# The query's row normalisation moved behind the third gate, its split behind the fourth Silu

## The chip, the cores and the metric

The kernel runs on one core of a Trainium2 chip. A core has five engines with queues of their own: TensorE (PE), VectorE (DVE), ScalarE (ACT), GpSimd (POOL) and SyncE (SP, here the queue of all DMAs). The metric is the device time of one execution in microseconds, the median of several runs. Lower is better.

## The reference

32 batches of `x` and of a context, each 256 x 512. For a batch:

```python
# attention-like mixing over channels; q is x with normalised rows
p = Wp @ q;  g = Wg @ ctx;  t = Wt @ ctx
att = sum over a group of 32 channels and all columns of p * g, * 0.125
u = Wz (per group) @ (att * t)
u = (u - mean) / sqrt(var + eps) * gamma + beta     # over a group
x1 = x + ctx + u
# feed-forward over rows; Q is blockwise FP4 quantisation, blocks of 16
n = layernorm(x1)
h = silu(Q(n) @ Q(w_gate).T) * (Q(n) @ Q(w_up).T)   # 512 -> 1408
out = x1 + Q(h) @ Q(w_down).T                       # 1408 -> 512
```

## The kernel before

The 256 rows of a batch (a "context", numbered i) make two tiles of 128 rows, the even one (s = 0) and the odd one (s = 1); tile j = 2i + s. After a stretch in which the weights are quantised, turned and split, the kernel is one loop over contexts, and each engine has the order of its work written out by hand in a function `body(i)`. Only semaphores join the engines. Each engine works strictly in its own order: an instruction that waits holds up all that stands behind it.

Products with more precision than one 16-bit pass are made of pieces: a matrix is split into a high part and a low part (`hi`, `lo`), and TensorE sums three products. The high part is made by ScalarE (a cast), the low part by VectorE or GpSimd (value minus high part).

What belongs to a tile j in `body`:

- TensorE: the scores of tile j + 2 (p, g, u), then the hidden product of tile j in four quarters of 352 columns, each gate and up side by side (L463), the group means (L450) and group spread of tile j + 2 between them, then the output product of tile j - 1 (L474).
- ScalarE: for each quarter the Silu (L711); between them moments of u, the split `c_hi` of the context after next (L630), `xm` (L640, an absolute value for the rounding), `x_hi` (L619), `q_hi` (L635), and behind the fourth Silu `affine`, which writes `v_sb` (L609).
- VectorE: a gate for each quarter (L916: Silu times up); the quantisation of the next tile's rows between the gates (`normalise2` L828, maximum L763, scale L766, reciprocal L839, `x_y` L742, then `x_finish` L751, L755, L759, and `x_lo` L906); `copy_group` L800 and `variance` L806 for the attention part; and in the odd tile `normalise1` (L785, two instructions, one for each half of the context after next), which writes `q`. Behind the fourth gate comes the quantisation of h: maximum L763, `h_scale` L766, small instructions up to L876, `h_y` L742; then `residual` L814, which needs `v_sb`, the statistics of x1, and `emit` L925.
- GpSimd: in the odd tile `ctx_lo` (`c_lo`, L1122), `columns` (five one-column instructions, L1136 to L1142, once `copy_group` is done), `q_lo` (L1128, once `q_hi` is done), `columns_affine` (five one-column instructions, L1146 to L1154, once `variance` is done, feeding `affine`), then `root2` and `add_ctx` (`xc`, L1117).

The semaphores that the moved work touches: `q_norm` (VectorE's L785; ScalarE's `q_hi` and the load of the next x wait for it), `q_hi_done` (GpSimd's `q_lo` waits), `q_ready` (TensorE's scores wait for `q_lo`).

Of the kernel before, what the change touches and what calls it, by code (L numbers as in the profile page):

```python
# [40 lines left out]
def at_least(eng, sem, n):  # L41

    if isinstance(n, int) and n <= 0:
        return
    eng.wait_ge(sem, n)
# [10 lines left out]
def build(nc, x, ctx_in, Wt, Wp, Wg, Wz, gamma, beta, w_gate, w_up, w_down, out):  # L56
# [18 lines left out]
    with ExitStack() as stack:  # L75
# [247 lines left out]
        def final_sets(c):  # L323

            return FINAL[2 * c:2 * c + 2]
# [257 lines left out]
        def _(act):  # L583
            def copy_p(t, pair):
                act.wait_ge(p_done, t + 1)
                at_least(act, pg_summed, t)
                nc.scalar.copy(p_sb[:, :], pairs[:, pair, 0, :]).then_inc(p_copied, 1)

            def copy_u(t):
                act.wait_ge(u_done, t + 1)  # L590
                at_least(act, v_ready, t)
                nc.scalar.activation(u_sb[:, :], ubank[:, :], ACT.Identity, accum_out=u_sum[:, 0:1]).then_inc(u_copied, 1)

            def u_moments(t):
                at_least(act, grp_done, t)
                at_least(act, sq_steps, 2 * t)
                act.wait_ge(u_copied, t + 1)
                nc.scalar.activation(rowst[:, 1:2], u_sum[:, 0:1], ACT.Identity, scale=-1.0 / D).then_inc(u_mean_made, 1)
                act.wait_ge(u_mean_made, t + 1)
                nc.scalar.activation(u_dev[:, :], u_sb[:, :], ACT.Square, bias=rowst[:, 1:2],  # L600
                                     accum_out=u_sum[:, 1:2]).then_inc(u_squared, 1)
                act.wait_ge(u_squared, t + 1)
                nc.scalar.activation(rowst[:, 2:3], u_sum[:, 1:2], ACT.Identity, scale=1.0 / D).then_inc(rowst_ready, 1)

            def affine(t):

                act.wait_ge(aff_steps, 8 * t + 8)
                at_least(act, x1_ready, t)
                nc.scalar.activation(v_sb[:, :], u_sb[:, :], ACT.Identity, bias=att[:, 10:11],  # L609
                                     scale=att[:, 8:9]).then_inc(v_ready, 1)  # L610
# [5 lines left out]
            def x_hi(t):  # L616
                act.wait_ge(xq_ready, t + 1)
                at_least(act, x_turned, 16 * t)
                nc.scalar.copy(xq_parts[:, 0, :], xq[:, :]).then_inc(x_hi_done, 1)  # L619

            def h_hi(j):
                at_least(act, h_turned, 16 * j)
                for r, (a, b) in enumerate(HPIECES):
                    act.wait_ge(hq_ready, 2 * j + r + 1)
                    nc.scalar.copy(hq_parts[:, 0, a:b], hq[:, a:b]).then_inc(h_hi_done, 1)  # L625

            def ctx_hi(b):
                act.wait_ge(c_loaded, 16 * b + 16)
                at_least(act, u_done, HT * b)
                nc.scalar.copy(c_parts[0][:, :, :], c_in[:, :, :]).then_inc(c_hi_done, 1)  # L630

            def q_hi(b):
                act.wait_ge(q_norm, HT * b + HT)
                at_least(act, p_done, HT * b)
                nc.scalar.copy(q_parts[0][:, :, :], q[:, :, :]).then_inc(q_hi_done, 1)  # L635

            def grain(m, y, y_done, count, done):

                act.wait_ge(y_done, count)
                nc.scalar.activation(m, y, ACT.Abs, scale=GRAIN).then_inc(done, 1)  # L640

            def weights_hi(weight_set):
                k, _, cols, dst = weight_set
                split_hi(dst[0], k % 2, len(cols), w_turned, k + 1, w_hi_done)
# [50 lines left out]
            def body(i):  # L695
                ahead = not isinstance(i, int) or i + 2 < NB
                more = not isinstance(i, int) or i + 1 < NB
                for s in range(HT):
                    j = HT * i + s
                    first = isinstance(j, int) and j == 0  # L700
                    if more and not first:
                        copy_p(j + 2, s)
                        copy_u(j + 2)
                    if not first:
                        h_hi(j - 1)
                    for c in range(GROUPS):
                        act.wait_ge(gu_done, GROUPS * j + c + 1)
                        at_least(act, h_done, GROUPS * j + c - 1)
                        if first and c == 0:
                            act.wait_ge(w_q_done, 3 * WCH - 1)  # L710
                        nc.scalar.activation(silu[:, c % 2, :], pairs[:, (s + 1 + c) % 2, 0, 0:GW], ACT.Silu,  # L711
                                             scale=w_unit[:, 0:1]).then_inc(silu_done, 1)
                        if first:
                            for one in final_sets(c):
                                weights_hi(one)
                        if c == 0 and more and not first:
                            u_moments(j + 2)
                        if c == 0 and ahead and s == 1:
                            ctx_hi(i + 2)
                        if c == 1 and (more or s == 0):  # L720
                            grain(xm[:, :], xn[:, :], x_y_done, j + 2, x_grain_done)
                        if c == 1 and ahead and s == 1:
                            q_hi(i + 2)
                        if c == 1 and (more or s == 0):
                            x_hi(j + 1)
                        if c == 3 and more:
                            affine(j + 2)
                    grain(hm[:, :], h[:, :], h_y_done, j + 1, h_grain_done)
# [10 lines left out]
        def _(dve):  # L739
# [143 lines left out]
            def h_snap_add(j):  # L883
                dve.wait_ge(h_grain_done, j + 1)
                snap_add(h[:, :], hm[:, :], h_t_done)

            def h_snap_back(j):
                dve.wait_ge(h_t_done, j + 1)
                snap_back(h[:, :], hm[:, :], h_r_done)
# [132 lines left out]
            def body(i):  # L1022
                more = not isinstance(i, int) or i + 1 < NB
                ahead = not isinstance(i, int) or i + 2 < NB
                for s in range(HT):
                    j = HT * i + s
                    t = j + 2
                    first = isinstance(j, int) and j == 0
                    quant_x = more or s == 0
                    if not first:  # L1030
                        h_snap_add(j - 1)
                        h_snap_back(j - 1)
                    if more:
                        sum_pg(t, s)
                    if not first:
                        h_finish(j - 1)
                        h_lo(j - 1)
                    for c in range(GROUPS):
                        gated(j, s, c)
                        if first:  # L1040
                            for k, _, cols, dst in final_sets(c):
                                split_lo(dst[1], dst[0], k % 2, len(cols), w_hi_done, k + 1, w_lo_done)
                        if c == 0 and quant_x:
                            normalise2(j + 1)
                            x_first(j + 1)
                            x_scales(j + 1)
                            x_y(j + 1)
                        if c == 0 and ahead and s == 1:
                            normalise1(i + 2)
                        if c == 1 and more:  # L1050
                            copy_group(t)
                        if c == 1 and quant_x:
                            x_finish(j + 1)
                        if c == 3 and more:
                            variance(t)
                        if c == 2 and quant_x:
                            x_lo(j + 1)
                        if c == 2 and ahead and s == 0:
                            ln1(i + 2)

                    h_first(j)
                    h_scales(j, s)
                    h_units(j, s)
                    h_y(j)
                    if more:
                        residual(t, s)
                        x1_moments(t)
                        x1_mean(t)
                    if not first:
                        emit(j - 1, 1 - s, 16 * (i - 1) if s == 0 else 16 * i)  # L1070
# [193 lines left out]
```

## Time and profile before

| what | value |
|---|---|
| median of 3 runs | 1893.15 us (1892.28 to 1893.98) |
| the profiled execution | 1893.97 us, span 1892.2 us |
| TensorE matmul busy | 1742.4 us (92%) |
| VectorE busy | 1656.3 us (88%) |
| GpSimd busy | 805.8 us (43%) |
| ScalarE busy | 719.6 us (38%) |
| mean granted TensorE clock | 0.978 of full speed |

The span is what the trace covers; the execution's time is 1.8 us more. A row of the timeline gives the start in microseconds from the span's start, the duration, the engine, the line in the kernel, the operation, the written tile, an arrow and the read tiles, and the shapes; "x2" is two like instructions in a row, given as one. In brackets stands how long the engine had been idle and what ended it. In the rows, `x` is the program's x1, and `att`, `ln_mv` and `ln_rs` lose their numbers. A waiting instruction is shown in two ways: where it waits for a semaphore there is idle time ahead of it, and where it has been issued and then can't go on, its own duration is longer.

### The profile page before, as it was taken

To read this page: it belongs to the slowest core of one execution; us is meant where nothing else is said; L and a number is where in the kernel's file an instruction comes from. 1 tells how busy PE (TensorE), PEld (TensorE's weight loads), DVE (VectorE), ACT (ScalarE), POOL (GpSimd) and SP (SyncE) were. 2 spreads that over 40 slices of the span, in tenths; PEclk is the share of its full clock that TensorE was granted. 3 is DMA by queue.
4 is the path that set the end of the run, shared out by engine and by line. 5 is a ranking of instruction groups with operands and counts; after the bars stand their busy time and mean duration, and the time that the engine had idled before them with its cause. 6 is when DMAs were issued, how large, how long until landed. Compare 5 with 4: busy or idle time off the path is not lost.

```text
span 1892.2 us, 30546 instructions
## 1 busy us (share of the span) xinstructions
PE 1742.4 (92%) x10062; PEld 1098.9 (58%) x10062; DVE 1656.3 (88%) x2629; ACT 719.6 (38%) x1237; POOL 805.8 (43%) x1065
## 2 busy tenths in 40 slices
PE   1537999999999999999999999999999999999996
PEld 1436566666666666666566666666566666666653
DVE  5585999999999999999999999999999999999984
ACT  2334434333344343433344343433434333433431
POOL 3648434344444434344444434434344444434400
PEclk9778999999999999999999999999999999999998
DMA  5100232322322232323222233222232233232222
GB/s 192 53 1 17 44 70 69 75 60 61 72 69 63 60 69 70 74 60 68 64 69 70 54 69 75 69 67 68 58 74 70 56 67 69 69 73 61 48 54 47
DMA packets 281879, 123.04 MB, mean 65 GB/s; under 512 B 252928, under 2 KB 254208, under 8 KB 281856
## 3 DMA queue, kind: packets, MB, share of 16 engines
q1 hardware_dynamic: 281856, 122.74, 27.4%
q8 instruction: 13, 0.21, 0.0%
q14 instruction: 10, 0.08, 0.0%
HBM read 43.03 MB, written 16.78 MB: 32 GB/s over the span
## 4 chain that ended last, share of the span: by engine, by line
PE 40%; DVE 35%; issue 16%; ACT 5%; POOL 2%; DVEq 1%; DMA 1%; ACTq 0%; SPq 0%; POOLq 0%
PE pairs L463 19%; PE obank L474 13%; PE pairs L442 4%; DVE hq L759 3%; DVE q L785 3%; DVE h L751 3%; DVE h L916 3%; DVE h L742 3%; ACT early L711 3%; DVE h_amax L763 3%; PE ubank L442 2%; DVE x L814 1%; ACT u_dev L600 1%; DVE ln_st L818 1%; DVE xn L755 1%
## 5 line engine op out<-in xcount | busy, mean ns | idle before, releaser
L463 PE MATMUL pairs<-w_gate_hi,xT_parts 128*128 128x352 f16 x2048 | 629.3, 313 | 16.1 <-DVE h L916 11.7
L463 PE MATMUL pairs<-w_up_hi,xT_parts 128*128 128x352 f16 x2048 | 628.4, 313 | 0.0
L474 PE MATMUL obank<-w_parts,hT_parts 128*128 128x512 f16 x2112 | 468.0, 380 | 12.9 <-DMA hT_parts<-raw 12.9
L474 PEld LDWEIGHTS obank<-w_parts,hT_parts 128*128 128x128 f16 x2112 | 207.5, 100 | 249.3 <-issue 15.9
L463 PE MATMUL pairs<-w_up_lo,xT_parts 128*128 128x352 f16 x1024 | 320.4, 313 | 0.0
L463 PE MATMUL pairs<-w_gate_lo,xT_parts 128*128 128x352 f16 x1024 | 320.3, 313 | 0.0
L463 PEld LDWEIGHTS pairs<-w_gate_hi,xT_parts 128*128 128x128 f16 x2048 | 205.3, 100 | 142.5 <-DVE h L916 23.3
L463 PEld LDWEIGHTS pairs<-w_up_hi,xT_parts 128*128 128x128 f16 x2048 | 200.6, 98 | 97.5
L916 DVE SCALAR_TENSOR_TENSOR h<-pairs,w_unit,early 128x352 f32<-128x352 f32 x256 | 148.1, 579 | 91.0 <-ACT early L711 90.9
L711 ACT ACTIVATE early<-pairs,w_unit 128x352 f32<-128x352 f32 x256 | 141.0, 551 | 86.6 <-PE pairs L463 86.6
L625 ACT CAST raw<-hq 128x704 f16<-128x704 f32 x128 | 99.6, 780 | 183.0 <-DVE hq L759 181.6
L1117 POOL TENSOR_TENSOR xc<-x_in,c_in 128x512 f32<-128x512 f32 x64 | 166.0, 2614 | 0.0
L1122 POOL TENSOR_TENSOR c_lo<-c_in,c_hi 128x512 fp32r<-128x512 f32 x64 | 95.2, 1508 | 161.3 <-ACT c_hi L630 154.3
L1136 POOL TENSOR_TENSOR att<-rowst,grp 128x1 f32<-128x1 f32 x64 | 40.4, 631 | 274.2 <-DVE grp L800 274.2
L640 ACT ACTIVATE hm<-h 128x1408 bf16<-128x1408 f32 x66 | 91.1, 1380 | 150.3 <-DVE h L742 150.3
L1158 POOL TENSOR_TENSOR ln_rs<-ln_mv,eps_col 128x1 f32<-128x1 f32 x64 | 14.9, 232 | 302.6 <-DVE ln_mv L822 302.6
L755 DVE SCALAR_TENSOR_TENSOR h<-hm,h 128x1408 f32<-128x1408 bf16 x66 | 138.2, 2094 | 2.2
L463 PEld LDWEIGHTS pairs<-w_up_lo,xT_parts 128*128 128x128 f16 x1024 | 100.2, 98 | 52.8
L463 PEld LDWEIGHTS pairs<-w_gate_lo,xT_parts 128*128 128x128 f16 x1024 | 100.2, 98 | 52.8
L609 ACT ACTIVATE v_sb<-u_sb,att 128x512 f32<-128x512 f32 x64 | 52.2, 815 | 205.2 <-POOL att L1154 205.2
L759 DVE SCALAR_TENSOR_TENSOR hq<-h,h_unit 128x704 f32<-128x704 f32 x128 | 121.9, 992 | 0.1
L901 DVE TENSOR_TENSOR raw<-hq,raw 128x704 f16<-128x704 f32 x128 | 108.5, 890 | 3.0
(163 smaller groups left out, 3023.6 us busy)
## 6 DMA issues: line engine op xcount, KB each, us to landing
x_in<-in_x SPq DMA_DIRECT2D x32, 512.0 KB, 3.4
c_in<-in_ctx SPq DMA_DIRECT2D x32, 512.0 KB, 3.5
out<-early SPq DMA_DIRECT2D x64, 256.0 KB, 2.1
raw<-in_L_ffn_w_down SPq DMA_DIRECT2D x2, 1408.0 KB, 8.8
raw<-in_L_ffn_w_gate SPq DMA_DIRECT2D x2, 1280.0 KB, 8.4
w_parts<-in_L_ffn_w_up SPq DMA_DIRECT2D x2, 1280.0 KB, 9.1
xT_parts<-raw SPq DMA_TRANSPOSE x64, 3.1
hT_parts<-raw SPq DMA_TRANSPOSE x64, 5.2
```

Source lines behind the costliest of these rows:

```text
L442: mm = pe.matmul(dst, wT[wpart][:, k, s * P:(s + 1) * P], src[part][:, k, :], start=(k == 0 and wpart == 0 and part == 0), stop=(k == HT - ...
L463: mm = pe.matmul(pairs[:, pair, n, 0:GW], xT[s][part][:, k, :], w1[n][wpart][:, k, c * GW:(c + 1) * GW], start=(k == 0 and part == 0 and w ...
L474: mm = pe.matmul(obank[:, :], hT[part][:, k, :], w2[wpart][:, k, :], start=(k == 0 and part == 0 and wpart == 0), stop=(k == KH - 1 and pa ...
L625: nc.scalar.copy(hq_parts[:, 0, a:b], hq[:, a:b]).then_inc(h_hi_done, 1)
L640: nc.scalar.activation(m, y, ACT.Abs, scale=GRAIN).then_inc(done, 1)
L711: nc.scalar.activation(silu[:, c % 2, :], pairs[:, (s + 1 + c) % 2, 0, 0:GW], ACT.Silu, scale=w_unit[:, 0:1]).then_inc(silu_done, 1)
L755: nc.vector.scalar_tensor_tensor(out=y, in0=m, scalar=GRAIN, in1=y, op0=ALU.max, op1=ALU.subtract).then_inc(done, 1)
L759: nc.vector.scalar_tensor_tensor(out=blocks(q_out), in0=blocks(y), scalar=-factor, in1=over_block(scale), op0=ALU.mult, op1=ALU.mult).then ...
L901: nc.vector.tensor_tensor(hq_parts[:, 1, a:b], hq[:, a:b], hq_parts[:, 0, a:b], ALU.subtract).then_inc(h_lo_done, 1)
L916: nc.vector.scalar_tensor_tensor(out=h[:, c * GW:(c + 1) * GW], in0=pairs[:, (s + 1 + c) % 2, 1, 0:GW], scalar=w_unit[:, 1:2], in1=silu[:, ...
L1117: nc.gpsimd.tensor_tensor(xc[:, s, :], x_in[:, s, :], c_in[:, s, :], ALU.add).then_inc(xc_ready, 1)
L1122: nc.gpsimd.tensor_tensor(c_parts[1][:, s, :], c_in[:, s, :], c_parts[0][:, s, :].bitcast(F32), ALU.subtract).then_inc(c_ready, 1)
```

## The change

Two conditions differ. In the odd tile VectorE's `normalise1` of the context after next is issued behind the third gate rather than the first, and ScalarE's `q_hi` behind the fourth Silu rather than the second.

```diff
@@ scalar, body(i), for each quarter c @@
                         if c == 1 and (more or s == 0):
                             grain(xm[:, :], xn[:, :], x_y_done, j + 2, x_grain_done)
-                        if c == 1 and ahead and s == 1:
+                        if c == 3 and ahead and s == 1:
                             q_hi(i + 2)
                         if c == 1 and (more or s == 0):
                             x_hi(j + 1)
@@ vector, body(i), for each quarter c @@
                             x_y(j + 1)
-                        if c == 0 and ahead and s == 1:
+                        if c == 2 and ahead and s == 1:
                             normalise1(i + 2)
                         if c == 1 and more:
                             copy_group(t)
```

VectorE in the odd tile (s = 1), from the scaling of the next rows (L742) to the fourth gate. Before:

```order
L742 SCALAR_TENSOR_TENSOR xn<-xn,x_rinv 128x512
L785 TENSOR_SCALAR q<-x_in,ln_mv,ln_rs 128x512 x2
L916 SCALAR_TENSOR_TENSOR h<-pairs,w_unit,early 128x352
L800 COPY grp<-ubank 128x3
L751 SCALAR_TENSOR_TENSOR xn<-xm,xn 128x512
L755 SCALAR_TENSOR_TENSOR xn<-xm,xn 128x512
L759 SCALAR_TENSOR_TENSOR xq<-xn,x_scale 128x512
L916 SCALAR_TENSOR_TENSOR h<-pairs,w_unit,early 128x352
L906 TENSOR_TENSOR raw<-xq,raw 128x512
L916 SCALAR_TENSOR_TENSOR h<-pairs,w_unit,early 128x352
```

And with the change (`early` holds the Silu, `pairs` are TensorE's PSUM banks):

```order
L742 SCALAR_TENSOR_TENSOR xn<-xn,x_rinv 128x512
L916 SCALAR_TENSOR_TENSOR h<-pairs,w_unit,early 128x352
L800 COPY grp<-ubank 128x3
L751 SCALAR_TENSOR_TENSOR xn<-xm,xn 128x512
L755 SCALAR_TENSOR_TENSOR xn<-xm,xn 128x512
L759 SCALAR_TENSOR_TENSOR xq<-xn,x_scale 128x512
L916 SCALAR_TENSOR_TENSOR h<-pairs,w_unit,early 128x352
L785 TENSOR_SCALAR q<-x_in,ln_mv,ln_rs 128x512 x2
L906 TENSOR_TENSOR raw<-xq,raw 128x512
L916 SCALAR_TENSOR_TENSOR h<-pairs,w_unit,early 128x352
```

The two L785 have passed the second and third gates and the three instructions of `x_finish`.

ScalarE in the same tile, from the second Silu on (L711; `raw<-xq` is `x_hi`). Before:

```order
L711 ACTIVATE early<-pairs,w_unit 128x352
L640 ACTIVATE xm<-xn 128x512
L635 CAST q_hi<-q 128x1024
L619 CAST raw<-xq 128x512
L711 ACTIVATE early<-pairs,w_unit 128x352 x2
L609 ACTIVATE v_sb<-u_sb,att 128x512
```

And with the change:

```order
L711 ACTIVATE early<-pairs,w_unit 128x352
L640 ACTIVATE xm<-xn 128x512
L619 CAST raw<-xq 128x512
L711 ACTIVATE early<-pairs,w_unit 128x352 x2
L635 CAST q_hi<-q 128x1024
L609 ACTIVATE v_sb<-u_sb,att 128x512
```

`q_hi` has passed `x_hi` and the last two Silus and stands next to `affine`. The orders of TensorE, GpSimd and SyncE are the same in both.

## Rows read from the trace of the kernel before

**Rows 1.** Timeline of VectorE: start us, us, engine, line, operation.
```profile
991.67 0.68 DVE L906 TENSOR_TENSOR raw<-xq,raw 128x512 f16<-128x512 f32 x1
...
1044.70 0.68 DVE L906 TENSOR_TENSOR raw<-xq,raw 128x512 f16<-128x512 f32 x1
```

**Rows 2.** Timeline of TensorE, fourth quarter of the odd tile.
```profile
1014.39 0.31 PE L463 MATMUL pairs<-w_gate_hi,xT_parts 128*128 128x352 f16 x1
1014.54 0.31 PE L463 MATMUL pairs<-w_up_hi,xT_parts 128*128 128x352 f16 x1
1015.17 0.32 PE L463 MATMUL pairs<-w_gate_hi,xT_parts 128*128 128x352 f16 x1 [0.32 <-DVE h L916]
```

**Rows 3.** Waits: engine and line, waited for, us, times, longest.
```profile
PE ubank L450 <- ACT rowst L603: 12.9, 30, 0.4
```

**Rows 4.** Timeline of VectorE in the odd tile.
```profile
1011.44 1.30 DVE L742 SCALAR_TENSOR_TENSOR xn<-xn,x_rinv 128x512 f32<-128x512 f32 x1
...
1012.66 1.95 DVE L785 TENSOR_SCALAR q<-x_in,ln_mv,ln_rs 128x512 f32<-128x512 f32 x2
...
1016.53 0.69 DVE L759 SCALAR_TENSOR_TENSOR xq<-xn,x_scale 128x512 f32<-128x512 f32 x1
...
1018.44 0.58 DVE L916 SCALAR_TENSOR_TENSOR h<-pairs,w_unit,early 128x352 f32<-128x352 f32 x1 [1.22 <-ACT early L711]
...
1018.94 1.62 DVE L906 TENSOR_TENSOR raw<-xq,raw 128x512 f16<-128x512 f32 x1
...
1020.49 0.57 DVE L916 SCALAR_TENSOR_TENSOR h<-pairs,w_unit,early 128x352 f32<-128x352 f32 x1
...
1022.75 0.22 DVE L766 TENSOR_SCALAR h_scale<-h_amax 128x88 f32<-128x88 f32 x1
...
1024.17 0.27 DVE L876 TENSOR_SCALAR h_unit<-h_scale,h_pow 128x88 f32<-128x88 f32 x1
...
1024.35 1.62 DVE L742 SCALAR_TENSOR_TENSOR h<-h,h_rinv 128x1408 f32<-128x1408 f32 x1
...
1025.89 0.68 DVE L814 TENSOR_TENSOR x<-v_sb,xc 128x512 f32 x1
```

**Rows 5.** Timeline of GpSimd in the odd tile.
```profile
1010.93 2.94 POOL L1122 TENSOR_TENSOR c_lo<-c_in,c_hi 128x512 fp32r<-128x512 f32 x2 [5.19 <-ACT c_hi L630]
...
1017.52 2.50 POOL L1128 TENSOR_TENSOR q_lo<-q,q_hi 128x512 fp32r<-128x512 f32 x2
...
1021.26 0.19 POOL L1146 TENSOR_TENSOR att<-att,eps_col 128x1 f32<-128x1 f32 x1 [1.25 <-DVE att L806]
...
1022.72 0.19 POOL L1154 TENSOR_TENSOR att<-gb,att 128x1 f32<-128x1 f32 x1
```

**Rows 6.** Line L785, all executions: ns min/median/max.
```profile
L785 DVE TENSOR_SCALAR q<-x_in,ln_mv,ln_rs x64: 533/542/1493, 7.1 to 1756.7; 128x512 f32<-128x512 f32 x64
```

**Rows 7.** Timeline of VectorE and GpSimd while the weights are prepared.
```profile
107.08 2.59 POOL L1182 TENSOR_TENSOR w_parts<-hq,w_scale 128x1408 f32<-128x1408 f32 x1
...
107.93 1.77 DVE L766 TENSOR_SCALAR x_scale<-x_amax 128x32 f32<-128x32 f32 x1
```

**Rows 8.** Timeline of VectorE and GpSimd, start of the odd tile.
```profile
1001.90 1.61 DVE L751 SCALAR_TENSOR_TENSOR h<-hm,h 128x1408 f32<-128x1408 bf16 x1
...
1001.92 1.65 POOL L1107 TENSOR_TENSOR ln_rs<-ln_mv,eps_col 128x2 f32<-128x2 f32 x1
```

**Rows 9.** Timeline of ScalarE in the odd tile.
```profile
1009.80 1.05 ACT L630 CAST c_hi<-c_in 128x1024 fp32r<-128x1024 f32 x1
...
1012.78 0.63 ACT L640 ACTIVATE xm<-xn 128x512 bf16<-128x512 f32 x1 [1.05 <-DVE xn L742]
...
1014.65 1.05 ACT L635 CAST q_hi<-q 128x1024 fp32r<-128x1024 f32 x1 [1.24 <-DVE q L785]
...
1018.96 0.56 ACT L711 ACTIVATE early<-pairs,w_unit 128x352 f32<-128x352 f32 x1 [0.55 <-PE pairs L463]
...
1022.95 0.82 ACT L609 ACTIVATE v_sb<-u_sb,att 128x512 f32<-128x512 f32 x1 [3.43 <-POOL att L1154]
```

## The prediction

> **What bounds the kernel now.** I read the busy shares first, then the waits, then the timelines of one pair of tiles engine by engine. TensorE is busy 92% of the span and looks like the bound, but a pair of tiles repeats to the hundredth every 53.03 us (the same VectorE instruction at 991.67 and 1044.70, [rows 1]), and in each pair TensorE stands still twice. At the odd tile's fourth hidden quarter it waits for a gate: matmuls start 0.15 apart, and this one 0.63 after its neighbour, so 0.48 is lost [rows 2]. At the even tile's group means it waits for ScalarE, 12.9 us in 30 waits, 0.43 each [rows 3]. So TensorE has 0.9 us a pair to spare. VectorE has none: the long idle stretch of its odd tile is 1.22 us, ahead of the third gate [rows 4], and that is its own product going through ScalarE and back (xq, x_hi, Silu, gate). VectorE's chain, with such round trips in it, sets the 53.03. The reader is to judge every edit by one number: when `residual` (L814, 1025.89 in [rows 4]) starts.
>
> **What stretches VectorE's chain.** Some of its instructions are longer here than elsewhere, always beside a large GpSimd instruction. L742 takes 1.30, the pair L785 takes 1.95 with the two c_lo on GpSimd (1010.93 to 1013.87); L906 takes 1.62 with q_lo (to 1020.02) [rows 4, 5]. Alone L906 takes 0.68 [rows 1] and one L785 0.54 [rows 6]. It is waiting, not slow running: L906 ends 0.54 behind the end of q_lo, its own 0.68 less 0.14. A tiny tensor_scalar on 128x32 waits too, 1.77 us beside L1182, and ends 0.03 behind its end [rows 7]. The reverse holds: a 128x2 add on GpSimd that came 0.02 behind L751 took 1.65 us and ended 0.05 behind it [rows 8], where one-column adds take 0.19 [rows 5]. Reductions, the reciprocals, and gates (one operand in PSUM) are not held: gate L916 takes 0.58 in the middle of q_lo.
>
> **The change part by part.** No instruction is added or removed. In 30 odd tiles (contexts 2 to 31) the two L785 go from behind `x_y` to behind the third gate on VectorE, and q_hi (L635) from behind xm to behind the fourth Silu on ScalarE. GpSimd's order is unchanged, but q_lo, which waits for q_hi, now stands between `columns` and `columns_affine` at another time. All times below are in the pair at 1008 us, [rows 4, 5, 9] for before.
> First, up to the third gate. The second gate and the group copy take the place of L785, from 1012.66. xm ends at 1013.41 as before, but L751 meets the second c_lo and ends 0.55 behind it, 1014.42. L755 starts 0.03 later, at 1014.45, takes 0.69 like L759, and L759 starts at 1015.17. From L759 to the third gate it is 1.91 us (1016.53 to 1018.44), so that gate is at 1017.08, 1.36 earlier. L785 x2 start 0.50 later, at 1017.58, with GpSimd idle: two of 0.54, each overlapped by 0.08 with the next instruction, 0.92 in all. L906 is at 1018.50, without q_lo beside it: 0.60 to the fourth gate, now at 1019.10, against 1020.49. TensorE's fourth quarter starts 0.48 earlier, so the fourth Silu runs from 1018.48 to 1019.04 and holds the gate up by nothing. So far 1.39 is won: 0.95 and 0.94 of stall gone, 0.5 lost to L751's wait for c_lo.
> Second, what it gives back. q_hi follows the fourth Silu: 1018.94 to 1019.98. GpSimd starts 0.08 behind its releaser (c_hi ends 1010.85, c_lo starts 1010.93), so q_lo runs 1020.06 to 1022.56, its second half from 1021.29. h_amax is a reduction and passes. h_scale (L766, 128x88) stands 2.26 behind the fourth gate, at 1021.36: 0.07 behind the start of that second half, and it is of the kind that waits. It ends at 1022.56 + 0.22 - 0.14 = 1022.64. From h_scale's end to h_y (L742) it is 1.38, so h_y starts at 1024.02, against 1024.35. Of 1.39 won, 0.33 is left.
> Third, `columns_affine`, five tiny GpSimd instructions, now follows q_lo: L1146 at 1022.52, L1154 1.46 later at 1023.98, over at 1024.17. h_y, 1.62 us with two operands in SBUF, is issued at 1024.02, and ahead of it L876 is running until 1024.11. So L1154 asks 0.04 ahead of h_y. I take it to get in, at a cost to h_y of 0.02. Then v_sb is ready at 1024.21 + 0.82 = 1025.03, and `residual` starts 1.54 behind h_y at 1025.58: 0.31 earlier than before.
> TensorE's spare 0.9 covers 0.31, and what follows `residual` moves as one block. 30 x 0.31 = 9.3 us. The profiled execution took 1893.97 (span 1892.2), so 1884.7; it lies 0.8 above the median, so the median goes from 1893.15 to 1883.9, say 1884.
> Costed at nothing: q_hi's absence ahead of x_hi (it ended at 1015.70, long before xq at 1017.22), the later end of q_lo (the score matmuls that read it stand behind a whole output product on TensorE; were that cover gone, its lateness of 2.5 us would count), the earlier x transpose. DMA and SyncE see no new wait. What no row shows is a group of one-column GpSimd instructions beside the one-column tensor_scalars of h_units; at worst each of five holds one up by its 0.19, 0.5 us a pair in all, at best by nothing. I take nothing, since L1154 beside h_scale in [rows 4, 5] (1022.72 and 1022.75) left it at 0.22.
>
> The Trainium skill (SBUF — State Buffer, "A bandwidth-pool intuition that's wrong (but worth ruling out)") says that a side kept out resumes about 115 ns behind the end of VectorE's instruction. The trace disagrees for these GpSimd instructions: the add ended 0.05 behind. By the page's figure a blocked L1154 would end 0.3 behind h_y and the first rival below would cost 0.9 a pair rather than 0.7, so 1921.
>
> **Rivals.**
> 1. L1154 loses to h_y (slower). Place: 1023.98 against 1024.02; it decides by 0.04 us. Then L1154 ends 0.05 behind h_y, at 1025.69, v_sb runs 1025.73 to 1026.55, and `residual`, which waits for it, starts at 1026.58: 0.7 later than before, and VectorE idles a microsecond. 30 x 0.70 = 21: 1914. For it: from the end of q_lo, h_y is 0.08 + 1.38 away and L1154 1.46 - 0.04; one of the five small instructions 0.05 slower and it is lost. Against: L876 holds the way for h_y as well, and the asker that waits has got in each time (the second c_lo between L742 and L785).
> A page's rule bears on this. The Trainium skill (SBUF — State Buffer, "SBUF: two separate sides") has the shared pair of ports go to whoever starts first, for the whole instruction. By that L1154 wins by 0.04, the 1884 above; a slip of 0.05 makes it 1914.
> 2. h_scale is ahead of q_lo's second half (slower). It needs h_scale 0.07 sooner or q_hi 0.07 later. Then h_scale ends at 1021.58, q_lo at 1022.73, and h_y starts at 1022.97, across the middle of `columns_affine`: L1148 or L1150 is held to 1024.6 and the rest follows it. v_sb would be over between 1026.0 and 1026.7, `residual` 0.2 to 0.8 late: 1899 to 1917, 1911 in the middle. Against: the fourth gate can't be earlier than its Silu allows (1019.07), and that Silu also sets q_hi, so both move together.
> 3. The small instructions eat the 0.31, or TensorE's and ScalarE's phases do: 1892.
> 4. h_scale isn't held at all and `columns_affine` isn't either (128x88 too short to matter): v_sb at 1025.03 lets `residual` start at 1025.06, 0.83 earlier: 1893.2 - 25 = 1868, inside TensorE's 0.9. Against: 128x32 was held for 1.77.
>
> **How the numbers follow.** Forecast 0.50, rival 1 0.28, rival 2 0.11, rival 3 0.07, rival 4 0.04. A change under 0.2% (3.8 us) can't be told from none here. Faster is the forecast and rival 4: 0.54. Slower is rivals 1 and 2, 0.38 after a little of rival 2 near zero. Same: 0.08. The forecast's own range is 1881 to 1888 (0.2 to 0.4 a pair). To hold eight in ten the range must reach over rival 1: 1881 to 1915, and leaves out rival 4, half of rival 2's top and some of the forecast's tail. The outcome is the same in all 30 pairs, since the pairs repeat to 0.01 us; one in the middle would mean that it isn't.
>
> **What would show it.** Right: L785 x2 at 1.00, L906 at 0.68, L751 in the odd tile about 1.0, h_scale in 30 tiles about 1.28 where it was 0.22, L742 on h at 1.62, L1154 at 0.19, no idle time of VectorE ahead of L814, TensorE's wait at L463 gone and that at L450 up from 0.43 to about 0.6. A pair would take 52.72. Wrong by rival 1: L1154 at 1.7 us and L814 waiting for v_sb, the pair 53.73. Wrong by rival 2: h_scale at 0.22 and L1148 or L1150 long. The forecast falls if a gap of 0.04 us, worked out from rows rounded to 0.01, has the other sign.

## The result, and the profile after

| | before | after |
|---|---|---|
| median of 4 runs, us | 1893.39 (1892.28 to 1893.98) | 1882.06 (1880.79 to 1884.71) |
| profiled execution, us (span) | 1893.97 (1892.2) | 1881.79 (1880.0) |
| one pair of tiles, us | 53.03 | 52.64 |

The changed kernel takes 0.9943 of the time before, with a 95% interval of 0.9925 to 0.996: 11.3 us faster, where 9.3 were forecast. The pair is 0.39 shorter, the same to 0.03 in every pair, and 30 x 0.39 = 11.7 accounts for it. In the experiments below, two runs that were disturbed and far longer are left out: one of before (2088.58 us, beside experiments 5 to 7) and one of experiment 6 (6413.45 us).

The busy row of the page after:

```profile
PE 1735.7 (92%) x10062; PEld 1099.8 (59%) x10062; DVE 1639.9 (87%) x2629; ACT 715.3 (38%) x1237; POOL 805.7 (43%) x1065
```

It tells little: it is the busy row of before but for a per cent, and names no stall. The timeline of VectorE in the odd tile tells it; this one stands 6.58 us earlier in the span than the rows of before (start us, us, engine, line, operation, and in brackets the idle time and its releaser).

```profile
1006.85 0.98 DVE L751 SCALAR_TENSOR_TENSOR xn<-xm,xn 128x512 f32<-128x512 bf16 x1
...
1010.50 0.58 DVE L916 SCALAR_TENSOR_TENSOR h<-pairs,w_unit,early 128x352 f32<-128x352 f32 x1 [1.22 <-ACT early L711]
1011.00 1.00 DVE L785 TENSOR_SCALAR q<-x_in,ln_mv,ln_rs 128x512 f32<-128x512 f32 x2
1011.91 0.69 DVE L906 TENSOR_TENSOR raw<-xq,raw 128x512 f16<-128x512 f32 x1
1012.51 0.58 DVE L916 SCALAR_TENSOR_TENSOR h<-pairs,w_unit,early 128x352 f32<-128x352 f32 x1
...
1014.78 1.23 DVE L766 TENSOR_SCALAR h_scale<-h_amax 128x88 f32<-128x88 f32 x1
...
1017.21 0.27 DVE L876 TENSOR_SCALAR h_unit<-h_scale,h_pow 128x88 f32<-128x88 f32 x1
1017.39 1.62 DVE L742 SCALAR_TENSOR_TENSOR h<-h,h_rinv 128x1408 f32<-128x1408 f32 x1
1018.94 0.68 DVE L814 TENSOR_TENSOR x<-v_sb,xc 128x512 f32 x1
```

Read against [rows 4]: the two L785 take 1.00 and no longer 1.95, L906 takes 0.69 and no longer 1.62. In their place L751 takes 0.98, and `h_scale` 1.23 where it took 0.22. From the fourth gate to `h_y` it was 3.86 us (1020.49 to 1024.35), and is now 4.88 (1012.51 to 1017.39): most of what the fourth gate won is given back in one instruction on 128x88.

The same stretch on GpSimd:

```profile
1013.46 2.49 POOL L1128 TENSOR_TENSOR q_lo<-q,q_hi 128x512 fp32r<-128x512 f32 x2 [3.83 <-ACT q_hi L635]
1015.90 0.19 POOL L1146 TENSOR_TENSOR att<-att,eps_col 128x1 f32<-128x1 f32 x1
...
1017.35 0.19 POOL L1154 TENSOR_TENSOR att<-gb,att 128x1 f32<-128x1 f32 x1
```

`q_lo` is over at 1015.95 and `h_scale` at 1016.01, 0.06 behind. L1154 starts 0.04 ahead of `h_y` and takes its 0.19: it got in. Its line shows the same for every tile (ns min/median/max):

```profile
L1154 POOL TENSOR_TENSOR att<-gb,att x64: 189/190/191, 88.7 to 1804.4; 128x1 f32<-128x1 f32 x64
```

And what TensorE waits for, the row that answers to [rows 3], and its wait for the gates, which came 31 times before:

```profile
PE ubank L450 <- ACT rowst L603: 16.1, 30, 0.6
PE pairs L463 <- DVE h L916: 2.2, 2, 1.4
```

The first wait rose from 0.43 to 0.54 a pair, and the one at L463 behind the third gate [rows 2] is gone. Of the 0.91 that the two showed together, the pair has become 0.39 shorter, and about 0.5 is left in one place.

### The profile page after: what moved, and what is told of

The parts are those of the page before. It is cut to its first block, busy times and chain, and to the rows that moved or that the text cites. A ratio compares the mean times of both kernels' runs of the same rounds, so it can differ in the third digit from the quotient of the medians.

```text
span 1880.0 us, 30546 instructions
## 1 busy us (share of the span) xinstructions
PE 1735.7 (92%) x10062; PEld 1099.8 (59%) x10062; DVE 1639.9 (87%) x2629; ACT 715.3 (38%) x1237; POOL 805.7 (43%) x1065
## 4 chain that ended last, share of the span: by engine, by line
PE 41%; DVE 36%; issue 13%; ACT 6%; POOL 2%; DVEq 1%; DMA 1%; ACTq 0%; SPq 0%; POOLq 0%
PE pairs L463 19%; PE obank L474 13%; PE pairs L442 5%; DVE hq L759 3%; DVE h L751 3%; DVE h L742 3%; ACT early L711 3%; DVE h_amax L763 3%; PE ubank L442 2%; DVE xn L742 2%; DVE h_scale L766 2%; DVE h L916 2%; DVE xn L751 2%; DVE q L785 2%; ACT u_dev L600 1%
## 5 line engine op out<-in xcount | busy, mean ns | idle before, releaser
L463 PE MATMUL pairs<-w_gate_hi,xT_parts 128*128 128x352 f16 x2048 | 628.4, 313 | 6.5 <-DVE p_sb L794 3.6
L463 PE MATMUL pairs<-w_up_hi,xT_parts 128*128 128x352 f16 x2048 | 627.9, 313 | 0.0
L463 PE MATMUL pairs<-w_gate_lo,xT_parts 128*128 128x352 f16 x1024 | 320.3, 313 | 0.0
L463 PE MATMUL pairs<-w_up_lo,xT_parts 128*128 128x352 f16 x1024 | 320.2, 313 | 0.0
L463 PEld LDWEIGHTS pairs<-w_gate_hi,xT_parts 128*128 128x128 f16 x2048 | 205.5, 100 | 123.6 <-issue 17.7
L463 PEld LDWEIGHTS pairs<-w_up_hi,xT_parts 128*128 128x128 f16 x2048 | 200.5, 98 | 98.8
L711 ACT ACTIVATE early<-pairs,w_unit 128x352 f32<-128x352 f32 x256 | 140.8, 550 | 113.0 <-PE pairs L463 113.0
L463 PEld LDWEIGHTS pairs<-w_up_lo,xT_parts 128*128 128x128 f16 x1024 | 100.2, 98 | 52.9
L463 PEld LDWEIGHTS pairs<-w_gate_lo,xT_parts 128*128 128x128 f16 x1024 | 100.2, 98 | 52.7
L1128 POOL TENSOR_TENSOR q_lo<-q,q_hi 128x512 fp32r<-128x512 f32 x64 | 79.7, 1266 | 114.6 <-ACT q_hi L635 114.6
L759 DVE SCALAR_TENSOR_TENSOR hq<-h,h_unit 128x704 f32<-128x704 f32 x128 | 121.8, 991 | 0.1
```

The source lines that it names most:

```text
L463: mm = pe.matmul(pairs[:, pair, n, 0:GW], xT[s][part][:, k, :], w1[n][wpart][:, k, c * GW:(c + 1) * GW], start=(k == 0 and part == 0 and w ...
L759: nc.vector.scalar_tensor_tensor(out=blocks(q_out), in0=blocks(y), scalar=-factor, in1=over_block(scale), op0=ALU.mult, op1=ALU.mult).then ...
```

## Experiments

Each is the changed kernel with one edit, unless it says otherwise. The time of before beside each is that of runs on the same chip.

| kernel | L785 in the odd tile | q_hi behind | pair, us | median, us | of the time before |
|---|---|---|---|---|---|
| before | first gate | second Silu and xm | 53.03 | 1893.39 | 1 |
| 1: q_hi alone moved | first gate | fourth Silu | 53.12 | 1897.24 | 1.0018 (1.0009 to 1.0027) |
| after | third gate | fourth Silu | 52.64 | 1882.06 | 0.9943 (0.9925 to 0.996) |
| 2: q_hi behind the third Silu | third gate | third Silu | 52.68 | 1883.33 | 0.9941 (0.9926 to 0.9957) |
| 8: L785 in the gap, q_hi late | ahead of the third gate | fourth Silu | 52.65 | 1883.32 | 0.9947 (0.993 to 0.9963) |
| 7: L785 in the gap, q_hi behind the third Silu | ahead of the third gate | third Silu | 51.87 | 1859.48 | 0.982 (0.9802 to 0.9837) |

**1. `q_hi` alone moved** (from the kernel before; the first line is before's):

```
-                        if c == 1 and ahead and s == 1:
+                        if c == 3 and ahead and s == 1:
                             q_hi(i + 2)
```

> The kernel before with q_hi alone moved behind the fourth Silu; normalise1 stays behind the first gate. Theory: L906 falls from 1.62 to 0.68, but h_scale meets q_lo and L785 keeps its 1.95: h_y starts 0.1 later than in the kernel before, 1893.4 + 3.5 = 1897, if L1154 still gets in ahead of h_y; 1920 or more if not. Rival, that the gain is ScalarE's doing (x_hi no longer behind q_hi): 1882 to 1890.

1897.24 us (1895.54 to 1899.61, 11 runs) against 1893.82. Its VectorE timeline:

```profile
1014.15 1.94 DVE L785 TENSOR_SCALAR q<-x_in,ln_mv,ln_rs 128x512 f32<-128x512 f32 x2
...
1020.42 0.68 DVE L906 TENSOR_TENSOR raw<-xq,raw 128x512 f16<-128x512 f32 x1
...
1023.30 1.25 DVE L766 TENSOR_SCALAR h_scale<-h_amax 128x88 f32<-128x88 f32 x1
```

L906 gains 0.94 and `h_scale` loses 1.03: one stall changed for another, 0.09 to the worse, as the 53.12 says. L785 still meets `c_lo`. So the gain of the whole change is that of moving L785: 53.12 - 52.64 = 0.48 a pair, about the 0.95 of its own stall less the 0.5 that L751 now waits, 0.45 by the prediction's terms. The other half, L785 alone behind the third gate, can't be run: `q_hi` would wait for it ahead of the third Silu, and the third gate, behind which it stands, waits for that Silu. So the 0.48 is a difference of two runs, not a measurement of its own.

**2. `q_hi` behind the third Silu**

```
-                        if c == 3 and ahead and s == 1:
+                        if c == 2 and ahead and s == 1:
                             q_hi(i + 2)
```

> The changed kernel, but q_hi behind the third Silu (normalise1 stays behind the third gate). Theory: q_hi waits for q and holds the fourth Silu and gate up by 1.07 us, but q_lo is over 0.2 ahead of h_scale, which no longer waits its 1.0: residual within 0.1 of the changed kernel's, 1884 (1881 to 1887), with h_scale at 0.22 and the fourth gate a microsecond later. Rival, that h_scale's wait costs nothing: the later gate counts in full, 1882 + 32 = 1914.

1883.33 us (1882.49 to 1883.49). VectorE, ScalarE and GpSimd in its odd tile:

```profile
1015.19 0.58 DVE L916 SCALAR_TENSOR_TENSOR h<-pairs,w_unit,early 128x352 f32<-128x352 f32 x1 [0.97 <-ACT early L711]
...
1017.46 0.21 DVE L766 TENSOR_SCALAR h_scale<-h_amax 128x88 f32<-128x88 f32 x1
```
```profile
1013.65 1.05 ACT L635 CAST q_hi<-q 128x1024 fp32r<-128x1024 f32 x1 [1.57 <-DVE q L785]
```
```profile
1014.78 2.49 POOL L1128 TENSOR_TENSOR q_lo<-q,q_hi 128x512 fp32r<-128x512 f32 x2 [3.53 <-ACT q_hi L635]
```

`h_scale` is free, since `q_lo` is over 0.19 ahead of it. But `q_hi` waits for the second L785 and then keeps ScalarE from the fourth Silu, so the fourth gate is an idle 0.97 late. The stall at `h_scale` is bought off with a wait at the gate, and the sum is the same to 0.04 a pair, as expected.

**3. One more one-column instruction on GpSimd, ahead of `columns_affine`**

```
+                        nc.gpsimd.tensor_tensor(att[:, 7:8], minus_half[:, 0:1], minus_half[:, 1:2], ALU.mult)
```

> The changed kernel with one more one-column instruction on GpSimd between q_lo and columns_affine in the odd tile (it multiplies two constants into an unused column). Theory: in the changed kernel L1154 gets the shared port 0.04 us ahead of h_y (L742, 128x1408); 0.15 us later it doesn't, ends behind h_y, v_sb comes 1.5 us later and residual (L814) waits for it: L1154 at about 1.6 us, L814 about 1.0 later, a pair 53.65 in place of 52.64, 1882 + 30 = 1912. Rival, that small GpSimd instructions aren't kept out and only the order of semaphores counts: v_sb comes 0.15 later, still 0.4 ahead of its reader, 1882.

1912.7 us (1912.12 to 1914.28), 1.01 of before (1.0085 to 1.0116), pair 53.65. VectorE and GpSimd:

```profile
1032.30 1.61 DVE L742 SCALAR_TENSOR_TENSOR h<-h,h_rinv 128x1408 f32<-128x1408 f32 x1
1034.85 0.69 DVE L814 TENSOR_TENSOR x<-v_sb,xc 128x512 f32 x1 [0.93 <-ACT v_sb L609]
```
```profile
1030.81 0.19 POOL L1230 TENSOR_TENSOR att<-minus_half 128x1 f32<-128x1 f32 x1
...
1032.40 1.56 POOL L1154 TENSOR_TENSOR att<-gb,att 128x1 f32<-128x1 f32 x1
```

An instruction of 0.19 us, on an engine that is busy 43% of the span, costs a microsecond a pair against the changed kernel: it puts L1154 0.10 behind `h_y`, which holds it to 1033.96 (0.05 behind its own end at 1033.91), and `residual` waits 0.93 for v_sb. This is the first rival as priced (53.73 forecast, 53.65 measured), and it did not happen in the changed kernel by a lead of 0.04.

**4 and 5. `q_hi` later by one or two one-column activations**

```
+                            for k in range(2):
+                                nc.scalar.activation(spare[:, k:k + 1], w_unit[:, 0:1], ACT.Identity, scale=1.0)
                             q_hi(i + 2)
```

With one:

> The changed kernel with one more one-column activation on ScalarE ahead of q_hi in the odd tile, so that q_hi and q_lo come 0.1 to 0.2 us later. Theory: h_scale then asks ahead of q_lo's second half and takes 0.22 in place of 1.23, h_y starts a microsecond earlier, across the middle of columns_affine, and L1148 or L1150 is held by it; residual comes 0.3 to 1.2 later than in the changed kernel: 1892 to 1917. Rival, that h_scale's wait is the only thing on the chain: a microsecond a pair is won up to TensorE's spare 0.5, about 1866. Second rival, nothing is that close: 1882.

With two:

> As with one activation ahead of q_hi (which moved q_lo by 0.09 us only and left q_lo's second half 0.02 ahead of h_scale), but two: q_lo comes 0.18 to 0.2 later than in the changed kernel, and its second half 0.07 to 0.1 behind h_scale. Theory: h_scale takes 0.22, h_y starts 1.0 earlier and crosses columns_affine, L1148 or L1150 is held by h_y, and residual waits for v_sb: 0.4 to 1.2 later than in the changed kernel, 1894 to 1918. Rival, that only h_scale's wait matters: 1866 to 1870. Second rival, no such threshold: 0.1 more than with one, 1890.

With one: 1886.89 us (1886.4 to 1887.33), pair 52.75. It moved `q_hi` by only 0.09 (the two overlap), and the time met none of the expectations: in 29 of 30 pairs `h_scale` was still held. In the first of them, the odd tile in which context 2 is split, `h_scale` started 0.02 ahead of `q_lo`'s second half, took 0.21, and `residual` waited 1.47.

```profile
1014.99 0.19 ACT L724 ACTIVATE spare<-w_unit 128x1 f32<-128x1 f32 x1
1015.08 1.03 ACT L636 CAST q_hi<-q 128x1024 fp32r<-128x1024 f32 x1
```
```profile
1017.44 1.31 DVE L768 TENSOR_SCALAR h_scale<-h_amax 128x88 f32<-128x88 f32 x1
```

With two: 1914.06 us (1910.11 to 1914.58) against 1893.18, ratio 1.0104 (1.0085 to 1.0122). Now the second rival's case is there, VectorE first and then GpSimd:

```profile
1031.87 0.20 DVE L769 TENSOR_SCALAR h_scale<-h_amax 128x88 f32<-128x88 f32 x1
...
1032.75 0.09 DVE L769 TENSOR_SCALAR h_row<-h_row 128x1 f32<-128x1 f32 x1
1032.89 0.15 DVE L750 TENSOR_SCALAR h_pow<-h_row 128x1 uint32<-128x1 uint32 x1
...
1033.46 1.62 DVE L745 SCALAR_TENSOR_TENSOR h<-h,h_rinv 128x1408 f32<-128x1408 f32 x1
1037.19 0.69 DVE L817 TENSOR_TENSOR x<-v_sb,xc 128x512 f32 x1 [2.11 <-ACT v_sb L610]
```
```profile
1030.73 2.50 POOL L1131 TENSOR_TENSOR q_lo<-q,q_hi 128x512 fp32r<-128x512 f32 x2 [4.01 <-ACT q_hi L636]
...
1033.45 2.05 POOL L1151 TENSOR_TENSOR att<-att,minus_half 128x1 f32<-128x1 f32 x1
```

`h_scale` is through in 0.20, so `h_y` comes a microsecond earlier behind the gate. It then meets the middle of `columns_affine` and holds L1151, the power of minus a half (L1148 in the changed kernel), which takes 2.05 us in place of 0.56. Everything behind it is late, and `residual` waits 2.11. **VectorE's stall went and the kernel became 32 us slower than the changed one.** In 22 of 30 pairs it is so (53.81 us). In 8 L1151 is free, but then the next instruction, L1153, is held, and `residual` waits 1.47 (53.20), as in this one of GpSimd and VectorE:

```profile
443.28 0.56 POOL L1151 TENSOR_TENSOR att<-att,minus_half 128x1 f32<-128x1 f32 x1
443.92 1.07 POOL L1153 TENSOR_TENSOR att<-att 128x1 f32<-128x1 f32 x1
```
```profile
443.31 1.63 DVE L745 SCALAR_TENSOR_TENSOR h<-h,h_rinv 128x1408 f32<-128x1408 f32 x1
```

**6. The second half of `q_lo` on 32 of its 512 columns** for contexts 2 and up (480 columns are left out of the computation):

```
-                    nc.gpsimd.tensor_tensor(q_parts[1][:, s, :], q[:, s, :], q_parts[0][:, s, :].bitcast(F32),
+                    n = 32 if s == 1 and not (isinstance(b, int) and b < 2) else D
+                    nc.gpsimd.tensor_tensor(q_parts[1][:, s, 0:n], q[:, s, 0:n], q_parts[0][:, s, 0:n].bitcast(F32),
```

> The changed kernel, but the second half of q_lo covers 32 of its 512 columns for contexts 2 to 31 (the other 480 keep old values: a part of the computation is left out). Theory: h_scale takes 0.22 in place of 1.23 and columns_affine is over before h_y, so VectorE could be a microsecond a pair faster, and TensorE's spare 0.5 (its wait at the group means) then sets the end: that wait gone, a pair 52.1, 1882 - 16 = 1866 (1863 to 1870). Rival, that h_scale's wait is not on the chain: 1882.

1860.19 us (1858.38 to 1861.04, 3 runs), ratio 0.9827 (0.9805 to 0.9848), pair 51.87. VectorE and GpSimd:

```profile
1003.31 0.24 DVE L766 TENSOR_SCALAR h_scale<-h_amax 128x88 f32<-128x88 f32 x1
```
```profile
1002.01 1.48 POOL L1129 TENSOR_TENSOR q_lo<-q,q_hi 128x512 fp32r<-128x512 f32 x2 [4.04 <-ACT q_hi L635]
...
1004.90 0.19 POOL L1155 TENSOR_TENSOR att<-gb,att 128x1 f32<-128x1 f32 x1
```

`h_scale` still starts behind the second half of `q_lo` and ends 0.06 behind its end (1003.55 against 1003.49), but that half now takes 0.25, so `h_scale` takes 0.24. The last of `columns_affine`, L1155 here, is not over ahead of `h_y`, as the expectation had it: it leads by 0.04, as in the changed kernel. No wait at L450 is left in TensorE's waits. So `q_lo` beside `h_scale` costs the changed kernel at least 0.77 a pair; more can't be seen, since TensorE is the new bound. The gain was larger than expected: the prediction let TensorE's 0.9 us cap it, and the cap lies at 53.03 - 51.87 = 1.16.

**7. L785 in VectorE's idle gap ahead of the third gate, `q_hi` behind the third Silu** (all of the computation):

```
-                        if c == 3 and ahead and s == 1:
+                        if c == 2 and ahead and s == 1:
                             q_hi(i + 2)
...
-                        if c == 2 and ahead and s == 1:
-                            normalise1(i + 2)
...
+                        if c == 1 and ahead and s == 1:
+                            normalise1(i + 2)
```

(the last two lines stand behind `x_finish`, which issues L759).

> normalise1 behind x_finish, ahead of the third gate, where VectorE idles 1.22 us for x_hi and the Silu; q_hi behind the third Silu. All of the computation. Theory: the pair L785 (0.92) fits into the idle time and the third gate stays where it is in the changed kernel; q_hi runs between the third and the fourth Silu, q_lo is over 0.6 us ahead of h_scale, so nothing is held, residual could start 1.4 earlier than before, and TensorE's spare 0.9 a pair sets the end: L450's wait gone, a pair 52.1, 1893.8 - 27 = 1867 (1864 to 1871). Rival, that the pair L785 costs its 0.9 wherever it stands, or that x_hi and the Silu come later by it: 1880 or more.

1859.48 us (1858.43 to 1860.19, 4 runs) against 1893.18: 0.982 (0.9802 to 0.9837), the fastest here that computes everything. VectorE, ScalarE and GpSimd:

```profile
1050.73 1.01 DVE L785 TENSOR_SCALAR q<-x_in,ln_mv,ln_rs 128x512 f32<-128x512 f32 x2
1052.03 0.58 DVE L916 SCALAR_TENSOR_TENSOR h<-pairs,w_unit,early 128x352 f32<-128x352 f32 x1 [0.29 <-ACT early L711]
...
1056.52 0.20 DVE L766 TENSOR_SCALAR h_scale<-h_amax 128x88 f32<-128x88 f32 x1
```
```profile
1051.89 1.03 ACT L635 CAST q_hi<-q 128x1024 fp32r<-128x1024 f32 x1
1053.66 0.55 ACT L711 ACTIVATE early<-pairs,w_unit 128x352 f32<-128x352 f32 x1 [0.73 <-PE pairs L463]
```
```profile
1053.01 2.56 POOL L1128 TENSOR_TENSOR q_lo<-q,q_hi 128x512 fp32r<-128x512 f32 x2 [1.67 <-ACT q_hi L635]
```

The two L785 lie in the 1.22 us in which VectorE waited anyway, and 0.29 of that is left. So `q` is ready for `q_hi` directly behind the third Silu, and ScalarE then still waits 0.73 for the fourth quarter, where in experiment 2 it kept VectorE waiting. `q_lo` is over 0.95 ahead of `h_scale`. A stretch of 106.1 us, about two pairs, from 1000 us on (window, us, then busy us of PE, PEld, DVE, ACT and POOL with counts, granted clock, DMA share, GB/s), first of the changed kernel and then of this one:

```profile
1000.00:1106.10 106.10, 105.01 (x611) 65.61 (x610) 97.37 (x162) 42.13 (x73) 45.87 (x64) 1.00 0.29 67
```
```profile
1000.00:1106.10 106.10, 106.10 (x621) 66.68 (x620) 95.95 (x162) 43.10 (x75) 47.70 (x65) 1.00 0.29 67
```

TensorE is busy for all of it, and its wait for ScalarE at L450 is gone: the bound has passed from VectorE's chain to TensorE, at the 51.87 us of experiment 6.

**8. L785 in the gap, `q_hi` late.** Experiment 7 made two edits. This one keeps L785 in the gap and leaves `q_hi` behind the fourth Silu:

```
-                        if c == 2 and ahead and s == 1:
-                            normalise1(i + 2)
...
+                        if c == 1 and ahead and s == 1:
+                            normalise1(i + 2)
```

> Half of the version that filled the idle time: normalise1 behind x_finish, in VectorE's idle time ahead of the third gate, but q_hi behind the fourth Silu as in the changed kernel. Theory: the fourth gate is then held by its Silu, 0.04 earlier than in the changed kernel, and all else stays: q_lo's second half is still 0.04 ahead of h_scale, which takes 1.2, h_y starts when it did: 1882 (1880 to 1884). If those 0.04 us are lost, h_scale goes first and the time is that of the two activations, 1900 to 1914. Rival, that it is the L785 in the idle time that gave 23 us, and not the time of q_lo: 1860.

1883.32 us (1882.03 to 1884.3) against 1892.49, pair 52.65. VectorE and GpSimd:

```profile
1014.44 0.58 DVE L916 SCALAR_TENSOR_TENSOR h<-pairs,w_unit,early 128x352 f32<-128x352 f32 x1 [0.80 <-ACT early L711]
...
1016.72 1.26 DVE L766 TENSOR_SCALAR h_scale<-h_amax 128x88 f32<-128x88 f32 x1
```
```profile
1015.42 2.49 POOL L1128 TENSOR_TENSOR q_lo<-q,q_hi 128x512 fp32r<-128x512 f32 x2 [3.65 <-ACT q_hi L635]
```

The 0.91 that the two L785 no longer take between the third and the fourth gate comes back as a wait of 0.80 for the fourth Silu, and `h_scale` is held as before. The gap alone brings nothing over the changed kernel, and `q_hi` behind the third Silu alone brings nothing (experiment 2); together they bring 23 us. Filling VectorE's idle time is only the means: it has `q` ready so early that `q_hi`, and with it `q_lo`, can go early without holding up the fourth Silu.

## Why the prediction was right, step by step

Times after are moved by 6.58 us, so that the first gates of the odd tile coincide.

| step | predicted | measured |
|---|---|---|
| L785 x2, behind the third gate | 1.00 | 1.00 |
| L906 | 0.68 | 0.69 |
| L751 | about 1.0 | 0.98 |
| third gate | 1017.08 | 1017.08 |
| fourth gate | 1019.10 | 1019.09 |
| q_lo starts | 1020.06 | 1020.04 |
| h_scale takes | 1.28 | 1.23 |
| h_scale ends | 1022.64 | 1022.59 |
| h_y starts | 1024.02 | 1023.97 |
| L1154 ahead of h_y | 0.04, gets in | 0.04, gets in |
| residual starts | 1025.58 | 1025.52 |
| pair | 52.72 | 52.64 |

The mechanism held, and the direction. Two terms were mis-sized.

**What residual gains**, 0.31 in the sum, measured 0.37 at `residual` and 0.39 in the pair. Of the first 0.06, 0.02 to 0.03 is that `q_lo` starts 0.02 sooner and takes 2.49, not 2.50. 0.02 is that `h_scale` ends 0.06 behind `q_lo`, not 0.08. Another 0.02 is the cost of L1154 to `h_y`, which the sum took from no row: `h_y` took 1.62 as before. Rounding takes 0.01 or so back. The last 0.02 of the pair builds up over the rest of it in steps under 0.01, and I could assign it to no instruction. Thirty times 0.08 is 2.4, against the 2.0 us between forecast and result.

**TensorE's spare**, 0.9 in the sum, is 1.16. It covered the gain of this change either way, so it cost the forecast nothing, but it set my expectations of experiments 6 and 7 6 to 8 us too high. What failed is the way of reading the wait at L450. The prediction read the one at L463 from starts (0.48) and this one from the idle time of the waits view (0.43). Starts give more, first before and then in experiment 7, where the wait is gone:

```profile
1037.24 0.31 PE L463 MATMUL pairs<-w_up_hi,xT_parts 128*128 128x352 f16 x1
1037.99 0.36 PE L450 MATMUL ubank<-rowst,gmean 128*128 128x3 f32 x2 [0.43 <-ACT rowst L603]
1038.20 0.31 PE L463 MATMUL pairs<-w_gate_hi,xT_parts 128*128 128x352 f16 x1
```
```profile
1020.08 0.31 PE L463 MATMUL pairs<-w_up_hi,xT_parts 128*128 128x352 f16 x1
1020.23 0.28 PE L450 MATMUL ubank<-rowst,gmean 128*128 128x3 f32 x2
1020.37 0.31 PE L463 MATMUL pairs<-w_gate_hi,xT_parts 128*128 128x352 f16 x1
```

From the matmul ahead of the group means to the one behind them it is 0.96 with the wait and 0.29 without: 0.67 lost, not 0.43. The idle time leaves out that a matmul that doesn't wait starts 0.15 behind its neighbour, while that one's 0.31 is still running. 0.48 and 0.67 make 1.15, and 1.16 was measured.

**The first rival** was real and near: experiment 3 makes it happen with 0.19 us of GpSimd work, at the price given (1914 forecast, 1912.7 measured). Its chance of 0.28 rested on a gap of 0.04 us taken from rows rounded to 0.01. The lead was there in all 30 pairs, 0.040 to 0.047, and L1154 got in each time. It is steadier than the prediction made it: as long as `q_lo` holds `h_scale`, both `h_y` and L1154 count from `q_lo`'s end, and wherever that end lies the lead is the same. It is 0.040 to 0.049 in every such pair of experiments 1, 4, 6 and 8 too. Experiment 3 changes it, since its work lies between the two. Experiment 5, where the power leads `h_y` by 0.00 to 0.03, is what a kernel looks like that stands on the edge itself.

**The second rival** was said to need `q_hi` 0.07 later, at a price of 1911 (1899 to 1917). Experiment 4 moved it by 0.09 and it came about in one pair of 30. The lead was larger than the 0.07 of the prediction: in the changed kernel the second half of `q_lo` starts at 1014.68 and `h_scale` at 1014.78, 0.10 later, and in experiment 4 0.02 of it is left in this pair (1017.42 against 1017.44) and 0.00 to 0.03 in the 29. Experiment 5 brought the rival about in all 30, at 1914. **The fourth rival** falls with `h_scale`'s 1.23. And the term taken at nothing for want of a row, VectorE's small instructions beside those of GpSimd, was nothing: from `h_scale`'s end to `h_y` it is 1.38 us (1016.01 to 1017.39), as before.

**The page's rule on the port.** The Trainium skill (SBUF — State Buffer, "SBUF: two separate sides") gives the pair of ports to whoever starts first. The traces of the changed kernel and of experiments 3 and 5 agree, down to about 0.03 us: L1154 passed 0.04 ahead and was held 0.10 behind, and the power passed with leads of 0.029 to 0.031. It was held in pairs in which it led by up to 0.022, which the rule alone doesn't give (see the last section). On how soon a side kept out resumes, the other section of that page named in the prediction has its figure from descriptors that GpSimd writes for a DMA; these compute instructions again differ: L1154 in experiment 3 ended 0.05 behind `h_y`, its own 0.19 included.

## What to carry to other kernels

When two engines share a port, don't ask which of them is overloaded; write down, for each large instruction of the one, which instruction of the other stands beside it, and put it beside those that don't ask (here gates with an operand in PSUM, reductions, reciprocals). A stall that is only moved comes back at the next instruction that asks, here at one of 0.2 us, and a stall that is taken away makes something else early, which can then hold a third: experiment 5 took a stall of 1 us a pair off VectorE and lost 32 us in all. So look for the place in which both the product and its reader fit, and change the two together: neither half of experiment 7 was worth anything alone (1883.33 and 1883.32 against 1882.06 us), and both together took 1859.48.

## What the runs showed of the hardware

- **The margin of a tie.** By the starts that the profile gives, the power on GpSimd led `h_y` in experiment 5 by up to 0.022 us in the pairs in which it was held and took 2.05, and by 0.029 to 0.031 in those in which it was not (0.56). The break is between 0.022 and 0.029 us of lead. Against `h_scale` any lead of `q_lo`'s second half was enough, from 0.000 us on in 29 pairs of experiment 4, and 0.023 behind it lost in the thirtieth; whether the difference is in `h_y`'s kind, or in the overlap of one GpSimd instruction with the next, stays open.
- **How wide an instruction must be to be held.** On GpSimd one column was enough: L1154 took 1.56 in place of 0.19 (experiment 3). On VectorE tensor_scalars on 88 and 32 columns were held (1.23 in place of 0.22, and 1.77 [rows 7]), but those on one column were not: in all 30 pairs of experiment 5 they took their 0.09 and 0.15 in the middle of `q_lo`'s second half. Widths between 1 and 32 were not run. A reduction (`h_amax`, 1.61 with and without `q_lo` beside it) and a reciprocal on 88 columns (0.69 in the same place) were not held either.
- **Small work is not free on an engine with idle time.** 0.19 us of GpSimd cost 1.01 us a pair, and two activations of 0.19 on ScalarE 1.17 in most pairs. One activation cost 0.11, since it overlapped with the next instruction and moved it by 0.09.
